# One block of a transformer on one core: GpSimd makes a query's low part ahead of two side tiles, and VectorE makes two value low parts ahead of a rotary sum

## The reference

```
h   = layernorm(x) * (1 + ca) + sa
q,k = rotary(h @ Wq + bq) * 128**-0.5, rotary(h @ Wk + bk);  v = h @ Wv + bv
x   = x + ga * (softmax(causal(q @ k.T)) @ v @ Wo + bo)
h   = layernorm(x) * (1 + cb) + sb
x   = x + gb * down(silu(gate(h)) * up(h))
rotary(t) = t * cos(pos) + rotate_half(t) * sin(pos)
```

## Time and profile before

| what | value |
|---|---|
| median of three runs | 1030.65 us (1030.63 to 1032.5) |
| the profiled execution's own time | 1031.39 us |
| its span in the profile | 1029.6 us |
| TensorE busy | 970.8 us, 94% |
| VectorE busy | 784.1 us, 76% |
| GpSimd busy | 764.7 us, 74% |
| ScalarE busy | 669.5 us, 65% |

### The profile page before, as it was taken

The page is one execution under the profiler, slowest core; times in us unless marked ns, Lnnn a source line. Parts: engine busy times, 40 slices in busy tenths (PEclk is TensorE's granted clock), DMA queues, the critical chain, the costliest instruction groups (busy, mean ns, idle before and its releaser), DMA issues.

```text
span 1029.6 us, 19698 instructions
## 1 busy us (share of the span) xinstructions
PE 970.8 (94%) x5853; PEld 854.3 (83%) x5853; DVE 784.1 (76%) x1605; ACT 669.5 (65%) x1385; POOL 764.7 (74%) x532
## 2 busy tenths in 40 slices
PE   6988999999999999999999999999999999998897
PEld 5877888888888888888888888888888788887787
DVE  6857877777788788877787778877887777877644
ACT  5756656676666666666666666666666567767763
POOL 3487877788778877787778878787778777885653
PEclk9999999999999999999999999999999999999999
DMA  7524443343334433443434333543344335431011
GB/s 248 166 79 139 118 118 101 107 131 114 102 101 139 127 113 111 138 127 100 115 97 141 103 111 97 148 127 107 107 142 124 109 99 159 139 103 42 1 42 42
DMA packets 86597, 116.74 MB, mean 113 GB/s; under 512 B 10468, under 2 KB 61732, under 8 KB 86564
## 3 DMA queue, kind: packets, MB, share of 16 engines
q1 hardware_dynamic: 86564, 116.33, 39.2%
HBM read 50.17 MB, written 32.57 MB: 80 GB/s over the span
## 4 chain that ended last, share of the span: by engine, by line
PE 62%; POOL 11%; issue 7%; DMA 7%; ACT 6%; DVE 4%; SPq 2%; ACTq 0%; POOLq 0%; DVEq 0%
PE ps_r L1504 13%; PE ps_r L1503 13%; PE ps_r L1502 13%; PE ps_s L1502 5%; PE ps_s L1504 4%; PE ps_s L1503 4%; PE ps_t L1663 4%; POOL swapped L734 3%; DMA swapped<-straight 3%; POOL qk_lo L744 3%; POOL straight L735 2%; DMA side_out<-squares 2%; DMA side_p<-side_out 2%; ACT straight L885 2%; ACT probs L1014 1%
## 5 line engine op out<-in xcount | busy, mean ns | idle before, releaser
L734 POOL TENSOR_TENSOR swapped<-swapped,sin_sb 128x512 f32<-128x512 f32 x124 | 167.5, 1351 | 135.5 <-DMA swapped<-straight 135.0
L1014 ACT ACTIVATE probs<-ps_s,neg_max 128x128 f32<-128x128 f32 (+7 forms) x256 | 190.2, 743 | 109.3 <-DVE neg_max L1394 109.3
L1394 DVE CUSTOM_DVE_ANT_0 ps_s<-ps_s,mask_wide 128x128 f32<-128x128 f32 (+7 forms) x256 | 193.4, 755 | 31.1 <-PE ps_s L1504 29.4
L744 POOL TENSOR_TENSOR qk_lo<-straight,qk_hi 128x512 fp32r<-128x512 f32 x124 | 161.8, 1315 | 63.3 <-ACT qk_hi L898 63.2
L1314 DVE TENSOR_TENSOR pT_lo<-ps_t,pT_hi 128x512 fp32r<-128x512 f32 (+3 forms) x260 | 126.7, 498 | 75.7 <-ACT pT_hi L992 75.6
L735 POOL TENSOR_TENSOR straight<-straight,cos_sb 128x512 f32<-128x512 f32 x124 | 181.8, 1466 | 0.0
L1235 DVE TENSOR_TENSOR straight<-straight,swapped 128x512 f32<-128x512 f32 x126 | 147.1, 1168 | 15.2 <-POOL straight L735 14.7
L754 POOL TENSOR_TENSOR pT_lo<-side_p,pT_hi 128x1024 fp32r<-128x1024 f32 (+1 forms) x62 | 150.9, 2434 | 0.0
L1502 PE MATMUL ps_s<-qk_hi 128*128 128x512 f32 (+4 forms) x384 | 139.8, 364 | 9.7 <-POOL qk_lo L744 9.5
L992 ACT ACTIVATE pT_hi<-ps_t 128x512 fp32r<-128x512 f32 (+3 forms) x260 | 117.1, 450 | 43.0 <-PE ps_t L1663 41.3
L1353 DVE SCALAR_TENSOR_TENSOR y<-ps_r,inv_sum,y 128x256 f32<-128x256 f32 x248 | 108.4, 479 | 35.7 <-PE ps_r L1504 31.7
(11 more groups left out here) (201 smaller groups left out, 2391.0 us busy)
## 6 DMA issues: line engine op xcount, KB each, us to landing
swapped<-straight SPq DMA_DIRECT2D x252, 128.0 KB, 2.3
side_out<-squares SPq DMA_DIRECT2D x31, 512.0 KB, 2.6
side_p<-side_out SPq DMA_DIRECT2D x124, 128.0 KB, 3.0
side_out<-squares SPq DMA_DIRECT2D x31, 448.0 KB, 2.5
side_p<-side_out SPq DMA_DIRECT2D x124, 112.0 KB, 2.5
x_in<-in_L_attn_x SPq DMA_DIRECT2D x4, 512.0 KB, 5.5
w_raw<-in_L_attn_Wk SPq DMA_DIRECT2D x8, 256.0 KB, 3.2
w_raw<-in_L_attn_Wq SPq DMA_DIRECT2D x8, 256.0 KB, 3.8
```

Of the source, the lines that this page charges most:

```text
L734: pool.tensor_tensor(swapped[:, q, :], swapped[:, q, :], sin_sb[:, cs], ALU.mult)
L744: pool.tensor_tensor(lo, rope_buffers(piece)[0][:, RANK[piece] % 2, :], hi.bitcast(F32), ALU.subtract)\
L1014: nc.scalar.activation(halved(t, probs[:, P_AT[step] * P:(P_AT[step] + t + 1) * P]), score_rows(step, t), ACT.Exp, bias=neg_max[:, t:t + 1 ...
L1394: nc.vector.tensor_tensor_reduce(rows, rows, halved(t, mask_wide[:, SEQ - n_keys:SEQ]), -1.0, -MASKED, ALU.add, ALU.min, accum_out=neg_max ...
```

## The change

Two tokens move. On GpSimd `low:Q1+` now stands ahead of `side:1`; on VectorE `low:V1` now stands ahead of `add:Q1+`. No instruction is added or removed, and the buffers and semaphores are the same.

```diff
 VECTOR_PLAN = """max:0 turn:6.0- turn:7.0- turn:7.1- max:1 low:P0- add:K0+ max:2 side:1 turn:0.0 add:Q0+ low:P1- max:3
         sum:W00- max:4 sum:W01- turn:2.0 sum:W10- side:3 max:5 sum:W11- add:K1+
-        turn:4.0 max:6 low:V0 add:Q1+ low:V1 max:7 turn:5.0 turn:5.1"""
-POOL_PLAN = """rotate:K0+ split:V rotate:Q0+ low:K0+ low:Q0+ rotate:K1+ split:K rotate:Q1+ split:Q low:K1+ side:1 low:Q1+
+        turn:4.0 max:6 low:V0 low:V1 add:Q1+ max:7 turn:5.0 turn:5.1"""
+POOL_PLAN = """rotate:K0+ split:V rotate:Q0+ low:K0+ low:Q0+ rotate:K1+ split:K rotate:Q1+ split:Q low:K1+ low:Q1+ side:1
         side:3 split:O"""
```

## The result

| | before | after |
|---|---|---|
| median | 1030.64 us (1029.67 to 1032.5, 4 runs) | 1071.97 us (1071.46 to 1072.67, 4 runs) |
| span of the profiled execution | 1029.6 us | 1069.6 us |

The ratio is 1.0399, with a 95% interval of 1.0381 to 1.0417. I had forecast 1057.0 us, with a range up to 1071: the direction and the place were right, the size was 41.3 us instead of 26.4.

A forecast was written before the change was run, and what follows sets the result against it. TensorE, busy 970.8 of 1029.6 us, was taken as the bound. Late rotations (18.5 us) plus late starts (7.8) gave 26.3 us on 1031.39: 1057.7, or 1057.0 against the median, range 1040 to 1071.

The forecast's parts named there:

- When `low:Q1+` can run: GpSimd, unit 12: it still waits for `high:Q1+` and starts about 409.03 us, as before; only unit 14 could win 2.1 us.
- The price of `side:1` in the new place: GpSimd, behind `low:Q1+`: 2.34 us a start, with no two-input VectorE sum beside it; the other end was 2.81.
- The stop before `P1-`: TensorE, unit 12: `P1-` waits for the end of `side:3`, 414.72 against 414.65 us, a stop of 0.1 us.
- The rotation and `K1+`, kinds 0 and 3: GpSimd's later rotation delays TensorE's `K1+`: 1.87 us late in unit 12 (kind 0), 0.67 us late in unit 15 (kind 3).
- Kind 1: Unit 13: rotations with `split:V` end at 448.83, then 0.03 + 1.32 us to `K1+`, which is 1.19 us late.
- the ring: Loop from `high:Q1+` through GpSimd's low part, side tiles, rotations, VectorE's sums and `low:P1-` to `K1+` and next `high:Q1+`.
- Kind 2: Unit 14: `K1+` at 477.14 us, 1.18 us early; TensorE alone could have been 2.25 us early.
- What a late start adds: VectorE starts `side:3` later after `K1+`, 6.26 instead of 5.98 us: 0.28 us in each of 28 units, 7.8 us.
- The second move: VectorE's `low:V1` ahead of `add:Q1+`: frees `Q0+` of 8.1 us of waits, delays the sum 0.68 us, adds nothing.
- The lateness wasn't absorbed: Rival at `low:P1-` and `K1+`: lateness is absorbed, only removed waits count, 15.8 us gained, or 1015 us; chance 0.07.
- The side tile didn't stay long: Rival on GpSimd: `side:1` stays long in its new place, 13.6 us more, 1071 us; chance 0.15.
- my own case: Late rotation plus late start lengthen the loop's passes: from 1045 to 1066 us, chance 0.73.

The follow-up runs named there:

- the run of kind 2 alone: GpSimd's move only in units with u % UNITS == 2, VectorE's everywhere, against the kernel before: 1030.48 us, ratio 1.0002; with VectorE as before 1030.34 us, ratio 0.9989.

## Why the prediction was right in its place and short in its size

**When `low:Q1+` can run.** Right. In unit 12 it starts 0.08 us behind its high part, 0.10 before. GpSimd's waits for a high part grew by 86.2 - 63.2 = 23 us, where I had named some 43 as a guide; `low:K1+` comes a microsecond later in kinds 0 and 3 and leaves less of the wait.

**The price of `side:1` in the new place.** Right: both side tiles take 4.47 us together. The lock that the Trainium skill states (SBUF — State Buffer, "SBUF: two separate sides") was read rightly for this instruction: no VectorE instruction with two SBUF inputs stands beside it any more in unit 12, and the two side tiles took 4.46 to 4.48 us in every unit.

**The stop before `P1-`.** Right in being small; it doesn't appear among the waits.

**The rotation and `K1+`, kinds 0 and 3.** Right: 29.76 against 29.64, and 28.40 against 28.43 us. Unit 29, which I let go as kind 3, is 0.8 us longer than forecast; that stays open.

**Kind 1: this is the step that failed.** "1.32 us from `add:Q0+`" to `K1+` was taken from unit 29, where GpSimd stood idle beside the sum. Behind `split:V` it doesn't. The row that I carried over had a condition, an idle GpSimd, that the new case lacks, and I had just used that very condition for `side:1`. It is worth 1.06 us of VectorE's time and 1.0 to 1.1 us a pass of the ring, 7 us in all; adding one wait gave it back. The 15.03 us of unit 13 were a short row too, some 0.15 us a unit.

**Kind 2.** Right without the clock (28.4 us against 28.43). I had not asked what a stop of 2 us does to TensorE's clock, and so put it at nothing: about 4 us in the profiled execution, and 1.1 for one late side tile.

**What a late start adds.** 0.28 us was right: `side:3` starts 6.23 us after `K1+` instead of 5.95, and the next `high:Q1+` ends 0.1 to 0.4 us later than before in most units (15.46 us after `K1+` in unit 13, 15.03 before). That the low part of `K1+` is a whole microsecond late as well was missed; the changed order hides it, and the old order of kind 3, in the run of kind 2 alone, doesn't.

**The second move.** I had it free of effect. With GpSimd's move that holds: 1073.3 without it, 1072.0 with it, and the two ranges overlap. Alone it costs 0.5%; that this comes of two stops brought together is read from one profile.

**The rivals.** The lateness wasn't absorbed: in kinds 0 and 3 it came out at `K1+` in full, within about 0.2 us of what was worked out, unit 29 aside. The side tile didn't stay long. That the time comes out near the 1071 us of that rival is chance: two costs that I hadn't listed came on top of my own case.

## What to carry to other kernels

When an instruction is moved ahead in one engine's order, look first at when its input is there: if it still has to wait, its old place cost nothing, and all that was moved behind the wait is late by the length of the wait, less what slack it had. Follow that lateness round the ring to the next iteration, and check each duration taken from another place for what stood beside it there. A stop of TensorE is to be priced with its clock, and two small stops close together may do what a long one does.

## What the runs showed of the hardware

- A VectorE sum with two SBUF operands (128 x 512) took 0.69 us alone and 1.73 us when a two-operand GpSimd instruction had begun 0.08 us earlier; making GpSimd wait for it was worth 7 of the 12 us of that run.
- After a stop of 2.14 us TensorE's granted clock fell to the lower level in three of seven cases (two of seven with GpSimd's move alone), after 2.8 us in six of seven, after 1.5 us at the same place in none (the changed kernel's profile). Behind two stops of 0.73 and 1.35 us, with 0.66 us of work between them, it fell in two of seven passes. A fall cost 1.3 to 1.6 us in most of these cases.
